# Where turned attention probabilities lie in PSUM, and which engine copies them out: one core, a macaron block in fp32

## The reference, cut to what matters

```python
x = x + 0.5 * ffn(layernorm(x)); x = x + attn(layernorm(x)); x = x + 0.5 * ffn(layernorm(x))

def ffn(x, Wq, Wk, Wv, Ws, Wd, Wo):       # H = 16 heads, DH = 64, E = 8 experts, top K = 2
    q, k = einsum('btc,hdc->bhtd', x, Wq), einsum('btc,hdc->bhtd', x, Wk)
    w, sel = top_k(einsum('btc,hec->bthe', x, Ws), 2)
    mix_v = einsum('bthk,bthke->bthe', sigmoid(w), one_hot(sel, E))
    v = einsum('bthe,bted->bhtd', mix_v, einsum('btc,edc->bted', x, Wv))
    probs = softmax(einsum('bhid,bhjd->bhij', q * DH ** -0.5, k))
    attn = einsum('bhij,bhjd->bihd', probs, v)
    _, sel_o = top_k(einsum('btc,hec->bthe', x, Wd), 2)
    mask_o = one_hot(sel_o, E).sum(axis=3)
    return einsum('bthe,bthd,efd->bthf', mask_o, attn, Wo).sum(axis=2)
```

## Time and profile before

| | |
|---|---|
| time, median of 3 runs | 2604.54 us (2603.84 to 2607.11) |
| the profiled execution | 2602.62 us, of it the span of instructions 2600.8 us |
| PE busy | 2476.2 us, 95% of the span |
| DVE busy | 2108.7 us, 81% |
| ACT busy | 1924.7 us, 74% |
| POOL busy | 1139.0 us, 44% |
| granted TensorE clock, mean over the span | 0.994 of full speed |

### The profile page before, as it was taken

The page is one execution under the profiler, slowest core; times in us unless marked ns, Lnnn a source line. Parts: engine busy times, 40 slices in busy tenths (PEclk is TensorE's granted clock), DMA queues, the critical chain, the costliest instruction groups (busy, mean ns, idle before and its releaser), DMA issues.

```text
span 2600.8 us, 111020 instructions
## 1 busy us (share of the span) xinstructions
PE 2476.2 (95%) x45824; PEld 2319.8 (89%) x45824; DVE 2108.7 (81%) x3498; ACT 1924.7 (74%) x6117; POOL 1139.0 (44%) x1126
## 2 busy tenths in 40 slices
PE   4999999999999999999999999999999999999997
PEld 3899999999899999999999899999999999999987
DVE  4788888888888888888888888888888888888874
ACT  3777777777777777777777777777777777777774
POOL 2344544434434444445345344444444453444431
PEclk8999999999999999999999999999999999999999
DMA  4555555565555655555655555556556556556553
GB/s 128 146 144 153 141 154 144 151 152 155 146 154 149 160 145 153 156 146 152 156 149 152 149 155 150 152 148 162 145 153 156 148 150 158 146 146 159 153 148 97
DMA packets 519346, 387.53 MB, mean 149 GB/s; under 512 B 214080, under 2 KB 436160, under 8 KB 510656
## 3 DMA queue, kind: packets, MB, share of 16 engines
q1 hardware_dynamic: 518416, 379.60, 54.6%
q10 hardware_dynamic: 432, 0.85, 0.1%
HBM read 191.64 MB, written 188.74 MB: 146 GB/s over the span
## 4 chain that ended last, share of the span: by engine, by line
PE 68%; ACT 15%; DVE 8%; issue 7%; POOL 1%; DMA 1%; SPq 0%; ACTq 0%; DVEq 0%; POOLq 0%
PE psT L451 14%; PE psS L408 14%; ACT PB L761 9%; PE psS L490 5%; PE psT L490 5%; PE psT L468 5%; PE psT L421 5%; PE psT L463 5%; PE psT L469 4%; PE psT L470 4%; DVE NMAX L639 4%; PE psT L435 4%; ACT PT L857 3%; ACT QK L770 1%; DVE QK L696 1%
## 5 line engine op out<-in xcount | busy, mean ns | idle before, releaser
L761 ACT ACTIVATE PB<-psS,NMAX 128x256 f32<-128x256 f32 x2048 | 951.4, 489 | 533.4 <-DVE NMAX L639 533.4
L639 DVE TENSOR_REDUCE NMAX<-psS 128x4 f32<-128x1024 f32 x512 | 602.1, 1217 | 79.8 <-PE psS L408 78.8
L451 PE MATMUL psT<-V,PT 128*64 128x64 f32 x16384 | 543.1, 224 | 18.1 <-issue 17.5
L451 PEld LDWEIGHTS psT<-V,PT 128*64 128x64 f32 x16384 | 503.3, 138 | 47.8 <-issue 22.7
L696 DVE TENSOR_TENSOR QK<-psT,QK 128x512 fp32r<-128x512 f32 x512 | 340.9, 688 | 177.0 <-ACT QK L770 174.9
L408 PE MATMUL psS<-QK 64*128 64x256 f32 x6144 | 434.9, 286 | 50.7 <-ACT PT L857 40.4
L408 PEld LDWEIGHTS psS<-QK 64*128 64x128 f32 x6144 | 389.8, 186 | 103.1 <-issue 100.6
L761 ACT ACTIVATION_READ_ACCUMULATOR PB<-psS,NMAX 128x1 f32 x2048 | 454.5, 222 | 0.0
L875 POOL TENSOR_TENSOR BT<-MT,diagv 128x1024 f32<-128x1024 f32 x128 | 307.8, 2405 | 115.3 <-DMA MT<-MIXd 115.3
L770 ACT ACTIVATE QK<-psT 128x512 fp32r<-128x512 f32 x512 | 295.6, 618 | 64.5 <-PE psT L470 49.5
L857 ACT ACTIVATE PT<-psS 128x512 f32<-128x512 f32 x512 | 286.4, 635 | 2.1 <-PE psS L490 1.9
(11 more groups left out here) (119 smaller groups left out, 4572.9 us busy)
## 6 DMA issues: line engine op xcount, KB each, us to landing
Vd<-VM SPq DMA_DIRECT2D x128, 512.0 KB, 3.7
V<-Vd SPq DMA_DIRECT2D x128, 512.0 KB, 5.3
AOd<-AO SPq DMA_DIRECT2D x256, 256.0 KB, 3.6
PJd<-PJ SPq DMA_DIRECT2D x64, 512.0 KB, 2.6
PR<-PJd SPq DMA_DIRECT2D x64, 512.0 KB, 4.1
MIXd<-MIX SPq DMA_DIRECT2D x64, 128.0 KB, 2.5
MT<-MIXd SPq DMA_DIRECT2D x64, 128.0 KB, 4.4
MASKd<-MASKR SPq DMA_DIRECT2D x64, 128.0 KB, 3.3
```

Of the source, the lines that this page charges most:

```text
L451: last = eng.matmul(M[64 * u:64 * u + 64, (t * NT + it) * DH:(t * NT + it + 1) * DH], PT[:, t, jt, cols], V[:, pm % 2, 4 * r + t, jt, :], ...
L639: eng.tensor_reduce(NMAX[:, ab, :, :], psS[:, ab, :, :, :], AX_X, ALU.max, negate=True).then_inc(s_max)
L761: eng.activation(PB[:, ab, j, it, :], psS[:, ab, j, it, :], ACT.Exp, bias=NMAX[:, ab, j, it:it + 1], accum_out=SUM[:, p % 2, it, 4 * r + t ...
```

## The change

All four turned heads now go into the banks of their own scores in `psS`; the ring holds none. The ring's list loses its two `turn` items a quarter, so that all later items sit at other places. One semaphore `s_turned` counts four turns a quarter, and there are four `s_copied`. `scores(n, 0)` waits for the copies of heads 0 and 1 of the quarter before, as it did, and `scores(n, 1)` now for those of heads 2 and 3.

The copies are dealt out anew: heads 0, 2 and 3 to ACT, head 1 to DVE. On ACT head 0's copy is put forward in quarters 0 and 3, directly behind the last exponentials and ahead of PJ, AQ, GS and AAT; in quarters 1 and 2 it stays with the others. On DVE head 1's copy stands in quarters 0 and 2 ahead of EQ and FW (EQ stood further ahead until now), in quarters 1 and 3 at the end, where head 3's was.

```diff
-            if works(n):
-                items += [("turn", n, t) for t in (2, 3)]
...
-            return psS[:, 0, t].rearrange("p n t -> p (n t)") if t < 2 else bank("turn", n, t)
+            return psS[:, t // 2, t % 2].rearrange("p n t -> p (n t)")
...
         def wait_turned(eng, n, t):
+            eng.wait_ge(s_turned, 4 * n + t + 1)
...
         def wait_copied(eng, n, t):
+            eng.wait_ge(s_copied[t], n + 1)
...
-                if n >= 1 and ab == 0:
-                    wait_copied(eng, n - 1, 0)
-                    wait_copied(eng, n - 1, 1)
+                if n >= 1:
+                    wait_copied(eng, n - 1, 2 * ab)
+                    wait_copied(eng, n - 1, 2 * ab + 1)
...
             def turn(n, t):
                 ab, j = divmod(t, 2)
-                if t >= 2:
-                    wait_vacant(eng, "turn", n, t)
                 eng.wait_ge(s_exp, 8 * n + 2 * t + 2)
...
-                last.then_inc(was_turned(n, t))
+                last.then_inc(s_turned)
...
+            def copy_second(n):
+                wait_turned(eng, n, 1)
+                wait_full(eng, "product", n - 1)
+                eng.tensor_copy(PT[:, 1].rearrange("p n t -> p (n t)"), turned(n, 1)).then_inc(s_copied[1])
...
-                if r == 2 and runs(q):
-                    equal(1, GM[:, :, :], at + 7)
-                if r == 0 and runs(q):
-                    equal(0, GS[:, :, :], at + 1)
...
+                if r in (0, 2) and works(n):
+                    copy_second(n)
                 if r == 0 and runs(q):
+                    equal(0, GS[:, :, :], at + 1)
                     weigh(at + 2)
                 if r == 2 and runs(q):
+                    equal(1, GM[:, :, :], at + 7)
                     weigh(at + 8)
...
-                if works(n):
-                    for t in (3,):
-                        wait_turned(eng, n, t)
-                        wait_full(eng, "product", n - 1)
-                        eng.tensor_copy(PT[:, t].rearrange("p n t -> p (n t)"), turned(n, t)).then_inc(was_copied(n, t))
+                if r in (1, 3) and works(n):
+                    copy_second(n)
...
+            def copy_turned(n, t):
+                wait_turned(eng, n, t)
+                wait_full(eng, "product", n - 1)
+                eng.activation(PT[:, t].rearrange("p n t -> p (n t)"), turned(n, t), ACT.Copy).then_inc(s_copied[t])
...
                     if works(n):
                         exponentials(n, 1, (1,))
+                        copy_turned(n, 0)
...
                 if works(n):
-                    for t in (0, 1, 2):
-                        wait_turned(eng, n, t)
-                        wait_full(eng, "product", n - 1)
-                        eng.activation(PT[:, t].rearrange("p n t -> p (n t)"), turned(n, t), ACT.Copy).then_inc(was_copied(n, t))
+                    if r in (1, 2):
+                        copy_turned(n, 0)
+                    copy_turned(n, 2)
+                    copy_turned(n, 3)
```

More of the change, by code:

```diff
@@ L217, in macaron_kernel @@
         s_turned = semaphore("s_turned")
-        s_copied = [semaphore(f"s_copied{i}") for i in range(2)]
+        s_copied = [semaphore(f"s_copied{i}") for i in range(4)]
         s_value = [semaphore(f"s_value{i}") for i in range(2)]
```

## The result

The changed kernel takes 2771.97 us in the median of 4 runs (2765.76 to 2778.78) against 2605.82 for the kernel before; the ratio is 1.0637 (95% interval 1.0606 to 1.0667). It is slower, as forecast, by 166 us where 121 were forecast, and 2 us above the upper end of the range. The profiled execution took 2778.78 us, with a span of 2775.7; it was the slowest of the four, so that the traces differ by 175 us and not by 166. One execution of the kernel before, of 5547.6 us where the others of its rounds took 2602 to 2605, was slow and is left out of all ratios.

What follows compares the result with a forecast made beforehand. TensorE bounds the kernel, busy 2476 of 2601 us. A pair of passes loses 4.2 us, x 26 = 109, plus 12 for other passes: +121 on 2602.6, 2724, with the median 1.9 above: 2725 us; range 2655 to 2770.

Steps and rivals of the forecast that it cites:

- 32.0: Joint of turning and scores ending quarter 0 of pass 32, a first half: second half of scores starts 0.2 us earlier.
- 32.1: Joint ending quarter 1 of pass 32: head 1's copy waits behind GM, itself held by POOL's MB; scores +2.1 us.
- 32.3: Joint ending quarter 3 of pass 32: ACT's head 3 ends at 2.75, second half of scores starts 0.15 us later.
- 33.0: Joint ending quarter 0 of pass 33, a second half: POOL's BT catches L716 or ST in two cases of three; mean +1.35 us.
- 33.1: Joint ending quarter 1 of pass 33: GM waits for MB again, but PE is later against POOL; +0.4 to +0.8, taken +0.5 us.
- 33.3: Joint ending quarter 3 of pass 33: with head 0 first on ACT, second half of scores starts 0.4 us earlier.
- PE busy near 2476 as before: the loss is all waiting: Sign to look for on TensorE: its busy time stays near 2476 us and all lost time is waiting.
- three cases in four: Chance that MT has landed and the lock strikes in quarter 0 of pass 32: 0.75 x 2.5 + 0.25 x 1.0 = +2.1 us.
- at 1 us each: The 12 passes outside the 26 repeated pairs, with less of the same losses: 12 us in all.
- rival 4: No change: gains in quarters 0 and 3 pay for quarters 1 and 2; rows make it 0.6 against 2.0 a pair; chance 0.05.
- rival 3: Faster, 2564 us: two engines copy heads 0 and 1 side by side, the 40.4 us wait for L857 goes; chance 0.07.
- Rival 2: Everything is caught by the DVE and POOL lock, in quarters 0 of both passes always: 2765 us; chance 0.14.

## Why the prediction was right in its mechanism and too low

Means over the 26 pairs, in us behind the start of turning; "start" is that of the second half of the scores, the last column the change of the whole quarter that follows:

| joint | forecast | start before | start after | change | quarter |
|---|---|---|---|---|---|
| 32.0 | -0.2 | 3.08 | 2.85 | -0.23 | -0.15 |
| 32.1 | +2.1 | 2.71 | 5.25 | +2.54 | +3.13 |
| 32.2 | +0.34 | 2.71 | 3.05 | +0.34 | +0.39 |
| 32.3 | +0.15 | 2.78 | 2.89 | +0.11 | +0.01 |
| 33.0 | +1.35 | 2.86 | 4.21 | +1.35 | +1.75 |
| 33.1 | +0.5 | 2.69 | 3.49 | +0.80 | +0.82 |
| 33.2 | +0.34 | 2.73 | 3.06 | +0.33 | -0.11 |
| 33.3 | -0.4 | 3.70 | 3.33 | -0.36 | -0.31 |
| a pair | 4.2 | | | 4.9 | 5.5 |

**Right:** the sign and the mechanism. Head 1's copy behind GM in quarter 1 and behind the residuals in quarter 2; the small gains of 32.0 and 33.3 and the small loss of 32.3 (each within 0.04 in its start); and the chain from EQ over NMAX and MB to GM and back to the scores. Moving the copy ahead of GM and holding BT, each alone, gave back 91 and 99 us. The rule quoted from the Trainium skill (SBUF — State Buffer, Who interferes with whom), that a DVE instruction with two SBUF inputs contends with a GpSimd instruction that reads SBUF, held for EQ too: 2.73 us in 32.0 where it takes 0.68 alone. In 33.0 S or ST was caught in 19 of 26 pairs, where two in three were assumed, and the mean came out as forecast.

**The step that failed:** "PE busy near 2476 as before: the loss is all waiting". The prediction took PE's instructions at their old lengths once the stall was over, and left TensorE's clock out of the sum. Of the 52 quarters behind 32.1 and 33.0, the 22 that hold a stretch at half clock grew by 1.1 and 1.3 us more than the start of their scores, in the mean; the other 30 grew by what the start had moved and no more (0.0 us). With two such quarters in passes 1 and 2 this is 29 us, the largest of the missing terms, and 29 us came back when PE was kept busy in the gaps. PE's busy time grew by 34 us in the quarters with such stretches; the rest of its 53 us I did not separate.

**Too low, first step:** "three cases in four" for the lock in 32.0. In 26 of 26 pairs an instruction of 32.0 was caught by BT, EQ in 23 and FW in 3 (the lengths are 2.5 us and more). 32.1 measured +2.54, within the step's own +2.3 to +2.6 for a caught case. 33.1 came out at its upper bound, +0.8. Together 0.7 us a pair, 19 us.

**Too low, second step:** "at 1 us each" for the 12 other passes. Their scores started 27 us later in all, 2.2 each: in the passes 1 to 8, where GM was held by MB as in 32.1, quarter 1 alone lost 0.7 to 3.6 us. That is 15 us more.

**The whole:** 29, 19 and 15 make 63. On the other side, pauses inside the product that name no releaser were 17.5 us before and 7.2 after, 10 less, most of it behind 33.2 (-0.44 us a pair against its start); what makes them was not tried. That leaves 53, and the trace lost 173 us from first to last turning where 121 were forecast, 52 more.

Two smaller errors: passes 58 to 61 are second halves all, so that only 24 of the 26 are pairs of the kind that was read (the other two lost 5.3 and 4.7 us, much like the mean of 5.5); and by the terms of the lower bound quarters 1 and 2 cost 2.3 us a pair, not the 2.0 set against 0.6 in rival 4, while the 0.7 left in rival 3 still holds the 0.5 of 33.0.

Rival 2, "everything is caught", came nearest in time, 2765 us, but by luck in part: 32.0 was always caught as it says, 33.0 was not, and the clock, which it leaves out as well, made up the difference. Rival 3's idea, that the wait for L857 can be won, was right for another change: it needs no DVE and no banks, only ACT's order.

## What to carry to other kernels

Before a copy that the bounding engine waits for is moved to another engine, read what stands in front of it there at each place, and whether a third engine can hold that: here DVE was less busy than PE, and still the scores started 0.3 to 2.5 us later in five of the eight joints. What is moved behind it counts as well, since it may slide into another engine's time. If a wait is for the last of several copies on one engine, first try to reorder that engine, only past what frees no buffer the waiting engine needs next: this gave 1.9% here, where the new banks and dealing cost 6.4%. When a change adds stalls to TensorE, ask for its clock behind them as well: here it was a sixth of the loss.

## What the runs showed of the hardware that had not been expected

An idle stretch of TensorE of 1.91 us (33.0) was followed by 3.4 us at half clock, though PE had been busy for 14.81 of the 15 us from 1445 to 1460, before it. It did not follow every stall: 24 times in the 64 passes. Of 26 stalls like that of 32.1 (2.5 us in the mean, nearly all of them equal) 14 were followed by such a stretch, and of 26 like that of 33.0 (1.4 us in the mean) 8; each stretch cost 1.1 to 1.3 us. With the gaps filled by 30 transposes a pair, 4 were left. What decides whether a given stall is followed by one was not tried.

GM gets in between two MB that POOL issues back to back, in 57 of 64 cases after and 59 of 64 before. In 32.1 after, the first MB ends at 1432.14, GM at 1432.69, and the second MB, where the first took 1.96 us, is drawn out:

```profile
1432.10 2.40 POOL L873 TENSOR_TENSOR MB<-MASKT,diago 128x1024 f32<-128x1024 f32 x1
```
